# Fused attention and layer norms on one core: TensorE's work ordered by pairs of tiles, softmax steps once a pair, weights in halves, a new order of the first pair

## What is computed

```python
# x: 8 sequences of 2048 tokens, 512 channels; 16 heads of 32 channels
        def proj(W, b):
            y = jnp.einsum('nse,fe->nsf', x, W) + b
            return y.reshape(n, s, h, d).transpose(0, 2, 1, 3)
...
        scores = jnp.einsum('nqhd,nkhd->nhqk', Q, K) * scale
        attn = jax.nn.softmax(scores, axis=-1)
        out = jnp.einsum('nhql,nlhd->nqhd', attn, V)
        out = out.reshape(n, s, e)
        return jnp.einsum('nse,fe->nsf', out, Wo) + bo
...
            cap = s_len // n_head
...
            yn = (y - mu) * jax.lax.rsqrt(var + 1e-05) * ln_g + ln_b
...
    x = x + _layernorm(_L0_attn_ref(_layernorm(x, axis=-1), ...), axis=-1)
    x = x + _layernorm(_L0_ffn_ref(_layernorm(x, axis=-1), ...), axis=-1)
```

## Time and profile before

| | us |
|---|---|
| median of three runs | 1724.89 |
| lowest and highest of them | 1721.78, 1727.76 |
| the profiled execution, its own time | 1726.47 |
| its span in the trace | 1724.7 |
| TensorE busy | 1657.1 |
| DVE busy | 1305.1 |
| POOL busy | 1287.8 |
| ACT busy | 863.9 |

### The profile page before, as it was taken

The page is one execution under the profiler, slowest core; times in us unless marked ns, Lnnn a source line. Parts: engine busy times, 40 slices in busy tenths (PEclk is TensorE's granted clock), DMA queues, the critical chain, the costliest instruction groups (busy, mean ns, idle before and its releaser), DMA issues.

```text
span 1724.7 us, 55416 instructions
## 1 busy us (share of the span) xinstructions
PE 1657.1 (96%) x22536; PEld 1322.6 (77%) x22536; DVE 1305.1 (76%) x2440; ACT 863.9 (50%) x1737; POOL 1287.8 (75%) x1295
## 2 busy tenths in 40 slices
PE   5899999999999999999999999999999999999992
PEld 4687887878878777787778878777877887877871
DVE  5677778778778778778778778778778778778774
ACT  3245445455455455445445455455455555554543
POOL 5377777778778778777778778778778778778766
PEclk9899999999999999999999999999999999999996
DMA  7556666666666666666666666666666666666541
GB/s 264 127 154 172 185 169 170 187 166 180 167 179 178 179 168 170 183 171 167 189 163 180 183 165 181 179 170 174 181 167 177 181 167 184 172 168 180 151 126 53
DMA packets 388630, 294.51 MB, mean 171 GB/s; under 512 B 296980, under 2 KB 296980, under 8 KB 387863
## 3 DMA queue, kind: packets, MB, share of 16 engines
q1 hardware_dynamic: 345366, 223.81, 49.1%
q10 hardware_dynamic: 43008, 67.15, 13.0%
HBM read 156.51 MB, written 67.24 MB: 130 GB/s over the span
## 4 chain that ended last, share of the span: by engine, by line
PE 93%; POOL 2%; issue 2%; DVE 1%; ACT 1%; DMA 1%; SPq 0%; ACTq 0%; POOLq 0%; DVEq 0%
PE ps_k L617 22%; PE ps_y L677 20%; PE ps_v L617 20%; PE ps_q L617 20%; PE ps_s L647 6%; PE ps_o L663 5%; POOL z L338 0%; POOL x_t L279 0%; DMA mr_row<-x_d 0%; DMA x_d<-mr 0%; POOL o_sb L353 0%; POOL probs L318 0%; DMA x_in<-in_xa 0%; POOL mr L272 0%; DVE stX L370 0%
## 5 line engine op out<-in xcount | busy, mean ns | idle before, releaser
L338 POOL TENSOR_TENSOR z<-z,b_row 128x512 f32<-128x512 f32 x128 | 193.7, 1534 | 236.8 <-DVE z L499 236.8
L579 ACT ACTIVATE q_sb<-ps_q,mr 128x512 f32<-128x512 f32 x128 | 88.1, 688 | 558.7 <-issue 558.7
L397 DVE STREAM_TRANSPOSE qT<-q_sb 128x512 f32<-128x512 f32 x128 | 137.6, 1075 | 112.2 <-ACT q_sb L579 111.6
L279 POOL TENSOR_TENSOR x_t<-x_t,mr_row 128x512 f32<-128x512 f32 x128 | 199.0, 1555 | 11.0 <-DMA mr_row<-x_d 8.0
L353 POOL TENSOR_TENSOR o_sb<-o_sb,x 128x512 f32<-128x512 f32 x128 | 162.2, 1286 | 34.9 <-ACT o_sb L514 34.9
L499 DVE TENSOR_TENSOR z<-z,g_row 128x512 f32<-128x512 f32 x128 | 88.6, 693 | 121.0 <-ACT z L514 120.1
L285 POOL TENSOR_TENSOR xT_lo<-x_t,xT_hi 128x512 fp32r<-128x512 f32 x128 | 168.2, 1314 | 7.6 <-ACT xT_hi L523 7.6
L318 POOL TENSOR_TENSOR probs<-probs,inv 128x512 f32<-128x512 f32 x128 | 136.0, 1063 | 47.8 <-DVE inv L451 47.8
L617 PE MATMUL ps_k<-wk_hi,xT_hi 128*128 128x512 f32 x512 | 155.5, 425 | 9.1 <-ACT wk_hi L532 9.1
L347 POOL TENSOR_TENSOR x<-x,res 128x512 f32<-128x512 f32 x128 | 163.1, 1295 | 0.5 <-ACT x L514 0.5
L677 PE MATMUL ps_y<-wo_hi,oT_hi 128*128 128x512 f32 x512 | 141.3, 397 | 7.8 <-DVE oT_lo L466 7.8
(11 more groups left out here) (86 smaller groups left out, 3698.9 us busy)
## 6 DMA issues: line engine op xcount, KB each, us to landing
x_t<-in_xt SPq DMA_DIRECT2D x64, 512.0 KB, 4.8
res<-in_xr SPq DMA_DIRECT2D x64, 512.0 KB, 5.1
k_bd<-kT SPq DMA_DIRECT2D x512, 64.0 KB, 2.4
v_d<-v_tok ACTq DMA_DIRECT2D x128, 256.0 KB, 2.2
v_key<-v_d SPq DMA_DIRECT2D x128, 256.0 KB, 3.8
p_bd<-pT ACTq DMA_DIRECT2D x512, 64.0 KB, 2.3
out<-o_sb SPq DMA_DIRECT2D x64, 512.0 KB, 3.0
x_in<-in_xa SPq DMA_DIRECT2D x63, 512.0 KB, 5.0
```

The costliest lines, as they stand in the source:

```text
L279: nc.gpsimd.tensor_tensor(x_t[v % 2][:, j, :, :], x_t[v % 2][:, j, :, :], mr_row[v % 2][:, :, 0, j].unsqueeze(1).to_broadcast([P, EC, P]), ...
L338: nc.gpsimd.tensor_tensor(z[:, j, :], z[:, j, :], b_row[:, :], ALU.add).then_inc(z_done, 1)
L397: nc.vector.transpose(qT[t % 2][:, :, :].rearrange("p n h -> p h n"), q_sb[:, :].rearrange("p (h d) -> p h d", d=D)).then_inc(qT_done, 1)
```

## The change

TensorE, SP, POOL, DVE and ACT now loop over pairs u. TensorE does scores of pair u-1 (128 small matmuls on the chip), mixed of pair u-2, then keys, queries, values of tile 2u, output of tile 2(u-2), and the same for tiles 2u+1 and 2(u-2)+1. The softmax steps, oT_hi and oT_lo are done once a pair, 1024 wide, and probs, pT, inv, oT_hi and oT_lo have one buffer in place of two of half the size. In DVE's loop the order from the gain of z on is: gain of z, k_turn(2u+1), x_moments(u+2), statistics of C, q_turn(2u+1); in POOL's it is x_root(u+2), bias of z, root of C, and at the top of the next turn the last addition of pair u-4. At the start weights are loaded, cast and split in halves, pair 0 is centred on DVE straight from PSUM, the row of means of pair 1 comes from matmuls too, tiles 0 and 1 use different PSUM banks, and keys of tiles 0 and 1 come before queries of tile 0.

```diff
+        order = "kqvo"
+        halves = (slice(0, 2), slice(2, 4))
+
+        k_bank, q_bank, v_bank = {1: ps_s[:, 0, :]}, {1: ps_s[:, 1, :]}, {1: ps_o[:, 0, :]}
...
+                if pair(u):
+                    keys_out(2 * u)
+                v = u + 3
+                if v < NV:
+                    sp.wait_ge(stats_done["X"], 2 * (v - 1))
+                    load_x(v)
+                if pair(u):
+                    keys_out(2 * u + 1)
+                v = u + 2
+                if v < NV:
+                    rows_of(v)
...
+            x_low(1)
+            x_root(1)
+            x_centre(2)
+            x_centre(3)
+
+            for u in range(NV + 4):
+                v = u - 4
+                if pair(v):
+                    for j in range(2):
+                        pool.wait_ge(lnz_done, 2 * v + j + 1)
+                        nc.gpsimd.tensor_tensor(o_sb[:, v % 2, j, :], o_sb[:, v % 2, j, :], x1[:, v % 3, j, :], ALU.add
+                                                ).then_inc(out_done, 1)
+                t = 2 * u + 1
+                if u >= 1 and tile(t):
+                    x_low(t)
+                v = u - 3
+                if pair(v):
                     root("A", v)
...
+                v = u - 1
+                if pair(v):
+                    pool.wait_ge(inv_done, v + 1)
...
+                                            ALU.mult).then_inc(norm_done, 1)
+                v = u - 3
+                if pair(v):
+                    root("B", v, 1.0 + EPS, EPS * EPS)
+                t = 2 * u + 3
+                if u >= 1 and tile(t):
+                    x_centre(t)
+                t = 2 * u + 2
+                if tile(t):
+                    x_low(t)
+                v = u + 2
+                if v < NV:
+                    x_root(v)
+                v = u - 3
+                if pair(v):
+                    if v == 0:
+                        pool.wait_ge(b_loaded, 3 * DMA)
+                    for j in range(2):
+                        pool.wait_ge(zg_done, 2 * v + j + 1)
+                        nc.gpsimd.tensor_tensor(z[:, j, :], z[:, j, :], b_row[:, :], ALU.add).then_inc(z_done, 1)
+                    root("C", v)
+
...
+            def first_centre(j):
+                dve.wait_ge(xt_loaded[0], DMA)
+                dve.wait_ge(rows_ready, 1)
+                nc.vector.tensor_tensor(x_t[0][:, j, :, :], x_t[0][:, j, :, :],
+                                        ps_y[:, j * P:(j + 1) * P].unsqueeze(1).to_broadcast([P, EC, P]), ALU.subtract
+                                        ).then_inc(first_centred, 1)
...
+            def y_in(t):
+                v, j = t // 2, t % 2
+                dve.wait_ge(y_ready, t + 1)
+                if t == 0:
+                    dve.wait_ge(b_loaded, 3 * DMA)
+                if v >= 3:
+                    dve.wait_ge(out_done, 2 * (v - 3) + j + 1)
+                nc.vector.tensor_tensor(x1[:, v % 3, j, :], ps_y[:, :], bo_row[:, :], ALU.add).then_inc(y_done, 1)
+                dve.wait_ge(y_done, t + 1)
+                if v:
+                    dve.wait_ge(aggr_done["A"], 2 * v)
+                nc.vector.bn_stats(st["A"][:, j, :], x1[:, v % 3, j, :]).then_inc(stats_done["A"], 1)
...
-            even_out("k")
-            even_out("q")
-            low(0, "k", wk_hi, wk_lo)
+            even_out("k", 0)
+            first_centre(0)
+            first_centre(1)
+            even_out("k", 1)
+            dve.wait_ge(xhi_done, 1)
+            nc.vector.tensor_tensor(xT_lo[0][:, :, :], x_t[0][:, 0, :, :], xT_hi[0][:, :, :].bitcast(F32), ALU.subtract
+                                    ).then_inc(first_low, 1)
+            low("k", 0, wk_hi, wk_lo)
...
+            low("q", 1, wq_hi, wq_lo)
             k_turn(0)
-            low(2, "v", wv_hi, wv_lo)
+            even_out("v", 0)
+            even_out("v", 1)
             q_turn(0)
-
-            for s in slots:
-                t = s - 3
+            low("v", 0, wv_hi, wv_lo)
+            low("v", 1, wv_hi, wv_lo)
+            k_turn(1)
+            q_turn(1)
+
+            for u in range(NV + 4):
+                t = 2 * (u - 3) + 1
                 if tile(t):
...
+                    y_in(t)
+                v = u - 1
+                if pair(v):
+                    scores = ps_s[:, :, :].rearrange("p r (i k) -> p r i k", k=H)
                     tops = top[:, :, :].rearrange("p (r i) u -> p r (i u)", r=2)
...
+                if pair(u - 3):
+                    moments("A", u - 3)
+                if pair(v):
+                    dve.wait_ge(top_done, v + 1)
+                    nc.vector.tensor_tensor(probs[:, :, :, :].rearrange("p (r i) u k -> p r (i u) k", r=2), scores,
+                                            tops.unsqueeze(3).to_broadcast([P, 2, 32, H]), ALU.subtract).then_inc(sub_done, 1)
+                v = u - 2
+                if pair(v):
+                    dve.wait_ge(ohi_done, v + 1)
+                    nc.vector.tensor_tensor(oT_lo[:, :, :, :].rearrange("p j a (r n) -> p r (j a) n", r=2),
+                                            ps_o[:, :, :].rearrange("p r (i n) -> p r i n", i=2 * EC),
+                                            oT_hi[:, :, :, :].rearrange("p j a (r n) -> p r (j a) n", r=2).bitcast(F32),
+                                            ALU.subtract).then_inc(olo_done, 1)
...
+                if 1 <= u < NV:
+                    k_turn(2 * u)
+                    q_turn(2 * u)
...
+                t = 2 * (u - 2)
+                if tile(t):
+                    y_in(t)
+                v = u - 3
+                if pair(v):
+                    for j in range(2):
+                        dve.wait_ge(lnx_done, 2 * v + j + 1)
+                        nc.vector.tensor_tensor(z[:, j, :], z[:, j, :], g_row[:, :], ALU.mult).then_inc(zg_done, 1)
+                if 1 <= u < NV:
+                    k_turn(2 * u + 1)
+                if u + 2 < NV:
+                    x_moments(u + 2)
+                v = u - 3
...
                         nc.vector.bn_stats(st["C"][:, j, :], z[:, j, :]).then_inc(stats_done["C"], 1)
-                        if j == 1:
-                            moments("C", v)
-                v = (s + 4) // 2
-                if s % 2 == 0 and 2 <= v < NV:
-                    x_moments(v)
-                t = s
-                if 1 <= t < NT:
-                    q_turn(t)
-                if s == 1:
-                    low(3, "o", wo_hi, wo_lo)
-                v = (s - 5) // 2
-                if s % 2 == 1 and pair(v):
-                    for j in range(2):
-                        dve.wait_ge(lnx_done, 2 * v + j + 1)
-                        nc.vector.tensor_tensor(z[:, j, :], z[:, j, :], g_row[:, :], ALU.mult).then_inc(zg_done, 1)
+                    moments("C", v)
+                if 1 <= u < NV:
+                    q_turn(2 * u + 1)
...
+                if pair(u):
+                    q_in(2 * u)
+                    v_in(2 * u)
+                if tile(2 * u + 2):
+                    x_high(2 * u + 2)
+                v = u - 3
+                if pair(v):
+                    shift("B", v)
+                    for j in range(2):
+                        scaled(z[:, j, :], x1[:, v % 3, j, :], "B", v, j).then_inc(lnx_done, 1)
+                v = u - 1
+                if pair(v):
+                    act.wait_ge(pT_done, v + 1)
+                    if v:
+                        act.wait_ge(o_ready, v)
...
+                        nc.scalar.dma_start(p_bd[rows, c % 2, :], pT[rows, :, :].rearrange("p n h -> p (n h)")).then_inc(p_moved, DMA)
+                if pair(u):
+                    q_in(2 * u + 1)
+                    v_in(2 * u + 1)
...
+            def scores(v):
+                pe.wait_ge(qT_done, 2 * v + 2)
+                for j in range(2):
+                    pe.wait_ge(k_moved[j], 4 * DMA * (v + 1))
+                if v:
+                    pe.wait_ge(sub_done, v)
+                for j in range(2):
...
+            def mixed(v):
+                pe.wait_ge(v_moved, DMA * (v + 1))
+                pe.wait_ge(p_moved, 4 * DMA * (v + 1))
+                if v:
+                    pe.wait_ge(olo_done, v)
...
+            def rows(v, part, to):
+                for i, q in enumerate(part):
+                    mm = nc.tensor.matmul(to[:, i * P:(i + 1) * P], mr[v][:, q // 2, q % 2:q % 2 + 1].to_broadcast([P, P]),
+                                          ident[:, :], start=True, stop=True)
+                mm.then_inc(rows_ready, 1)
+
             pe.wait_ge(consts, 7)
+            pe.wait_ge(aggr_done["X"], 2)
+            rows(0, (0, 1), ps_y)
             pe.wait_ge(root_done["X"], 1)
-            for q in range(4):
-                mm = nc.tensor.matmul(ps_y[:, q * P:(q + 1) * P], mr[0][:, q // 2, q % 2:q % 2 + 1].to_broadcast([P, P]), ident[:, :],
...
+            rows(0, (2, 3), ps_o[:, 1, :])
+            keys(0)
+            keys(1)
+            queries(0)
```

(30 more changed lines are left out.)

580 lines of the change are left out of this document (266 added, 314 removed).

## The result

The changed kernel takes **1890.93 us** in the median of 4 runs (1880.26 to 1895.65); the kernel before 1725.72 (4 runs). The ratio is 1.0952, 95% interval 1.0901 to 1.1002: 165 us slower, where I forecast 46 us slower and allowed up to 82. The profiled execution has a span of 1878.5 us and is the fastest of the four; the other three have a lower mean granted clock (0.964 to 0.967, against 0.970), so the clock probably fell more often in them. One of the four runs of the changed kernel with only the transpose of qT moved (experiment 4), 1955.4 us at a granted clock of 0.83, was in a slower state of the chip and is left out of its median.

What follows compares the result with a forecast made beforehand. TensorE was taken to bound the kernel, busy 1657.1 of 1724.7 us. Start 80, 61 pairs 1625.4 and end 64.2 summed to a 1769.6 span, 1771.4 with the 1.8 around it; forecast 1772 us, range 1745 to 1808.

Steps and rivals of the forecast that it cites:

- TensorE alone: Steady loop: a pair takes 25.34 us against 25.66 for two slots, a gain of 0.32 if TensorE never waits.
- small gaps: Steady loop over 122 slots: 7.7 us of gaps that are not waits for other engines, kept in the forecast.
- The wait for qT: Every pair: scores wait for a DVE and POOL chain of 9.75 us against TensorE's 8.49; 1.26 late, 1.2 taken.
- the overlaps: In the chain to qT: steps of one engine overlap by up to 0.08 at three places, giving a 1.0 wait.
- Rival 3, the clock: Loop: TensorE's waits drop its clock to 1.2 GHz; 1934 us if every wait does, 1850 at half; chance 0.07.
- The row of 1.41: Evidence against the clock falling: after a wait of 1.41 us the first group took 1.20, as in the steady loop.
- Start, 80 for the end of values of tile 5: Start: values of tile 5 end at about 80 us (75 to 87), 22.5 earlier than 102.5.
- scores of pair 1 need its keys moved, near 54: Start: keys of tile 3 end at 51.5, and scores of pair 1 come near 54 us once they are moved.
- 22.5 and 3.5 for the clock: Start: 22.5 us from scores of pair 1 to 76.5, then about 80 with stretches at the lower clock.
- End, 64.2 from values of tile 127: End: 64.2 us from values of tile 127 to the end of the span, 15.0 more than 49.2.
- The three passes: End: three passes through A, B and C after output 123, taking 18.3, 17.3 and 17.3 us.
- 61 pairs, 1625.4: Steady loop: 61 pairs at 26.54, less one 1.2 wait, plus 7.7 of gaps: 1625.4 us, 52.5 more than 1572.95.

Runs made afterwards that it cites:

- experiment 4: Changed kernel with qT's transpose ahead of stC on VectorE: 1858.2 us; also with 12 even-tile keys matmuls between scores and mixed: 1755.0; with 8: 1758.9.
- experiment 1: Changed kernel with the even tile's 12 large keys matmuls between scores and mixed: 1853.3 us; with only the first 4 there: 1807.2 us.
- experiment 5: Kernel with both edits, SyncE issuing g_row, b_row, res behind the keys' stores: 1749.0 us; then mixed moved mid-pair: 1744.0; then last pairs reordered: 1735.5.
- both edits: Changed kernel with 12 even-tile keys matmuls between scores and mixed, and the odd queries' transpose ahead of stC on VectorE: 1755.0 us.
- the kernel with the border held still: Changed kernel with 28 spare small matmuls a pair between keys and queries of the odd tile: 1910.3 us.

## Why the prediction was wrong

The direction was right, the size was not: 1772 forecast, 1890.93 measured, above the range. By its steps, against the profiled execution:

- **TensorE alone, 25.34 us a pair**: 25.60 measured. 16 us more over 61 pairs, of which I had put 7.7 down as small gaps. **The step that failed is the word "alone":** "no matmul goes", so I counted switches and took the run of 256 small matmuls to last 2 x 128 of them. The stalls inside it are 115 us, more than the whole forecast change. The row that bore on it was on the page of before, and I passed over it:

```profile
q8 instruction: 178, 2.92, 0.7%
```

  Packets of 16.4 KB, 256 instructions each by the count of matmuls and loads, beside a burst of 512 instructions should have made me ask how long one lasts.
- **The wait for qT, 1.26 by the rows, 1.2 taken**: the chain is there, in the forecast order, but 8.84 us long instead of 9.75. From the timeline of VectorE and GpSimd:

```profile
874.90 1.09 PE L707 MATMUL ps_q<-wq_hi,xT_hi 128*128 128x512 f32 x4
875.10 1.07 DVE L432 STREAM_TRANSPOSE kT<-ps_k 128x512 f32<-128x512 f32 x1 [0.19 <-PE ps_k L707]
...
876.02 1.23 DVE L401 BATCH_NORM_STATS2 stX<-x_in 128x6 f32<-128x512 f32 x2
...
877.89 1.32 POOL L293 TENSOR_TENSOR mr<-veX,x_powers 128x6 f32<-128x6 f32 x1
...
879.18 2.55 POOL L381 TENSOR_TENSOR z<-z,b_row 128x512 f32<-128x512 f32 x2
...
882.66 1.03 DVE L439 STREAM_TRANSPOSE qT<-q_sb 128x512 f32<-128x512 f32 x1
```

  From queries at 874.90 to scores at 883.74 there are 8.84 us. The two additions of z take 2.55, not 3.04 (the row of before held 3.04 for two), and the overlaps that I had given at most 0.25 give 0.4. So 0.28 of wait in 59 pairs. That is 56 us less than forecast, and it is not a free gain: without the stall, and with mixed 2.8 us later, the same chain costs 1.9 a pair (experiment 1), because VectorE then comes late to the keys' transpose, which I had bounded at 1.5 in all.
- **Rival 3, the clock**, had 0.07. It gives 1850 to 1934 and the time fell there, but by another road: it needs waits for qT to stop TensorE, and the falls stand behind the stalls, in 16 of 61 pairs, 25 us in all. That the time lies in its range is luck. The Trainium skill ("TensorE: Matmul & The Clock Gate", "HAM oscillation — how this bites in real kernels") tells of bursts parted by waits that lose the clock in every turn; here it was lost in 16 of 61, behind stalls of 1.70 to 2.42 us. The row of 1.41 us without loss fits: in the loops no pause under 1.67 us was followed by a fall.
- **Start, 80 for the end of values of tile 5**: 92.1. The failed step is "scores of pair 1 need its keys moved, near 54": they came at 65.03.

```profile
40.58 6.85 SPq L248 DMA_DIRECT2D g_row<-in_ln_g  x1
...
54.57 2.54 SPq L202 DMA_DIRECT2D k_bd<-kT  x4
...
65.03 1.28 PE L742 MATMUL ps_s<-k_bd,qT 64*32 64x64 f32 x73 [8.45 <-DMA k_bd<-kT]
```

  SyncE is held for 6.85 us in the issue of g_row, ahead of the keys' stores, and scores wait 8.45 us. From 65.03 to the end of values of tile 5 pass 27.1 us, where the forecast had 22.5 and 3.5 for the clock: 2.4 are the first stall and 1.9 the lower clock, which held until 73.2. Moving two rows and two loads gave 6 us back (experiment 5). It need not be g_row itself that holds SyncE: with it moved away, the issue of x_t at 40.66 took 5.67 us. What holds SyncE there stays open.
- **End, 64.2 from values of tile 127**: 68.4. The three passes are right; a stall of 1.99 and outputs at the lower clock behind a wait of 2.37 are the difference.
- **61 pairs, 1625.4**: 1718.0. 115 of stalls and 25 of clock more, 56 less for qT, 8 for the rest.

What an engineer could have read: the Trainium skill ("Runtime: NRT & Kernel Launch", "Instruction fetch mechanics") says that each engine's instructions are refilled in blocks of 16 KiB, 256 instructions, while the current one executes, and that crossing a border is mostly hidden. The traces agree with the block (16.4 KB, a border every 256 instructions, held still by 57 added ones). They disagree with the second half where 256 instructions last less than the 3.0 to 4.1 us above: by that sentence the runs of small matmuls would have cost nothing more, and they cost 119 us. The same section gives TensorE room for 2048 instructions in one sentence and speaks of only two blocks in another; a stall at the second border of a burst, 256 instructions behind the first, shows no such depth as 2048.

## What to carry to other kernels

Count instructions, not only busy time: where small matmuls follow each other so fast that 256 instructions (128 small matmuls with their loads here) last 1.3 us, a second such stretch right behind the first stalls TensorE by 2 us, and only large matmuls between them hide it (8.4 us left 8 of 119 us of stalls, 2.8 us left 20). A stall that is "issue" and whose place moves evenly from turn to turn is the sign of it. When a stall is removed, look at what it was hiding: here 1.9 us a pair of VectorE's chain came out, and moving one transpose removed that wait.

## What the runs showed of the hardware

- The time from one border to the next packet being usable was 3.0 to 4.1 us in the loop of the changed kernel, and sometimes longer (19.7 us of issue were left with 4.1 us of work between the borders). It has two parts. The packet of the instruction queue started 0.7 to 1.9 us after the border, and TensorE went on 2.15 to 2.8 us after that start, in all 63 stalls of the changed kernel. With both edits (experiment 4) the packet started up to 3.4 us after the border: the long fetches are mostly late starts. Why a packet starts late, and why it takes over 2 us to be usable, stays open.
- In the loops the clock fell behind pauses of 1.67 us or more and behind no shorter one, but not each time: in the kernel with the border held still, the same stall at the same place was followed by a fall in 24 of 61 pairs, and pauses of 1.67 and of 2.27 us are among them as well as among the others. What decides it stays open. A fall costs 1.55 us a pair.
- 128 more small matmul instructions a slot cost their work and two switches where they stood apart (119 us for 125 slots: 0.68 us of matmuls, and 0.27 that I put down to switches), and 142 us more where they stood next to the burst.
